# Eight matmuls without a use taken out of TensorE's queue between attention and experts, in a vision-tower kernel

## The reference, cut to what matters

```
h = tok(x)                                   # conv patches, local attention, class query: (64, 5, 256)
h = concat([cls_tok, h], axis=1)             # six tokens
h = h + attn(layernorm(h))                   # 16 heads, causal, ALiBi
x2 = layernorm(h)
logits = x2 @ gate_w                         # 8 experts, top 2
hidden = silu(x2 @ gate_w_e) * (x2 @ up_w_e) # for every expert e
h = h + sum over the top two of p_e * (hidden_e @ down_w_e)
```

## Time and profile before

| what | value |
|---|---|
| median of 3 runs | 247.56 us |
| the runs | 247.16, 247.56, 248.78 us |
| profiled execution: span, first to last instruction | 245.7 us |
| median less that span: what lies around it | 1.9 us |
| mean granted TensorE clock over the span | 0.971 |
| TensorE busy / its weight loads | 203.7 / 187.4 us |
| VectorE, ScalarE, GpSimd busy | 169.6, 105.8, 98.2 us |

### The profile page before, as it was taken

One profiled execution on the slowest core, in us unless ns is written; L12 is line 12 of the kernel. 1 busy time (PEld: TensorE's weight loads), 2 busy tenths in 40 slices (PEclk: granted clock), 3 DMA queues, 4 the chain that ended last, 5 costly groups with the idle time before them and its releaser, 6 DMA issues.

```text
span 245.7 us, 3903 instructions
## 1 busy us (share of the span) xinstructions
PE 203.7 (83%) x1320; PEld 187.4 (76%) x1320; DVE 169.6 (69%) x365; ACT 105.8 (43%) x230; POOL 98.2 (40%) x99
## 2 busy tenths in 40 slices
PE   0279899499999794687868899999999999999950
PEld 0279888379898574565646789999999999999950
DVE  0454895988464899967888769497857695948420
ACT  2153875172626560434321147364728372534200
POOL 0003879939414296337446404243322341514000
PEclk9999999859999997999999999999999999999996
DMA  6749933000930000000000001553543336000031
GB/s 198 239 125 365 379 153 128 23 1 0 366 149 0 0 1 3 0 0 0 1 0 3 0 0 40 220 184 98 234 124 132 104 152 236 20 0 0 3 18 46
DMA packets 5494, 23.01 MB, mean 94 GB/s; under 512 B 454, under 2 KB 3176, under 8 KB 4328
## 3 DMA queue, kind: packets, MB, share of 16 engines
q1 hardware_dynamic: 3746, 21.20, 24.6%
q10 hardware_dynamic: 1734, 1.63, 2.1%
HBM read 22.44 MB, written 0.39 MB: 93 GB/s over the span
## 4 chain that ended last, share of the span: by engine, by line
PE 57%; DVE 18%; issue 8%; POOL 5%; DMA 4%; ACT 3%; ACTq 1%; DVEq 0%; POOLq 0%
PE bank L720 22%; PE bank L733 14%; PE bank L420 8%; DMA raw<-xb 4%; PE bank L473 4%; DVE kv_rows L1191 2%; PE bank L610 2%; DVE vprod L344 2%; POOL rstd L1003 2%; POOL split L1032 2%; DVE normed L1160 1%; PE bank L619 1%; POOL window L1017 1%; DVE stats L1146 1%; PE bank L442 1%
## 5 line engine op out<-in xcount | busy, mean ns | idle before, releaser
L720 PE MATMUL bank<-split 128*128 128x322 f32 x384 | 59.2, 314 | 0.6 <-DVE normed L1517 0.6
L720 PEld LDWEIGHTS bank<-split 128*128 128x128 f32 x384 | 57.6, 188 | 0.9 <-issue 0.9
L1131 POOL TENSOR_TENSOR split<-raw,split 128x256 fp32r<-128x256 f32 x32 | 28.9, 905 | 56.7 <-DVE split L1470 56.7
L733 PE MATMUL bank<-split 128*128 128x256 f32 x288 | 36.1, 283 | 0.6 <-DVE split L1523 0.6
L733 PEld LDWEIGHTS bank<-split 128*128 128x128 f32 x288 | 35.4, 192 | 0.8 <-DVE split L1523 0.8
L420 PE MATMUL bank<-split 128*128 128x256 f32 (+1 forms) x255 | 34.0, 295 | 2.1 <-DVE split L1260 1.3
L420 PEld LDWEIGHTS bank<-split 128*128 128x128 f32 (+1 forms) x255 | 32.8, 203 | 2.6 <-issue 1.6
L473 PE MATMUL bank<-split 128*128 128x512 f32 x108 | 28.3, 417 | 0.4 <-DVE split L1292 0.4
L473 PEld LDWEIGHTS bank<-split 128*128 128x128 f32 x108 | 21.2, 201 | 5.0 <-DVE split L1292 0.7
L974 ACT ACTIVATE normed<-bank 128x322 f32<-128x322 f32 x32 | 13.9, 436 | 23.6 <-PE bank L720 23.6
L1517 DVE TENSOR_TENSOR normed<-bank,normed 128x322 f32<-128x322 f32 x32 | 15.7, 491 | 11.3 <-PE bank L720 8.0
(11 more groups left out here) (164 smaller groups left out, 292.8 us busy)
## 6 DMA issues: line engine op xcount, KB each, us to landing
raw<-ffn_w SPq DMA_DIRECT2D x8, 1536.0 KB, 6.5
raw<-xa SPq DMA_DIRECT2D x5, 768.0 KB
tok<-tok_w SPq DMA_DIRECT2D x1, 1536.0 KB, 11.9
tok<-tok_w SPq DMA_DIRECT2D x1, 776.0 KB, 7.5
raw<-xb SPq DMA_DIRECT2D x5, 114.0 KB
raw<-conv_w SPq DMA_DIRECT2D x1, 512.0 KB
raw<-xa ACTq DMA_DIRECT2D x1, 512.0 KB
att<-att_w SPq DMA_DIRECT2D x1, 488.0 KB, 12.7
```

What stands on the lines that cost most here:

```text
L720: mm = pe.matmul(bank[b][:, 0:NCOL], aws[:, q, pw, a:a + P], ms[:, px, c, FIRST:ROWS], start=(c == 0 and m == 0), stop=(c == CC - 1 and m ...
L733: mm = pe.matmul(bank[b][:, 0:C], hids[:, px, s * FQ + q, a:a + P], bws[:, s, pw, q * C:(q + 1) * C], start=(q == 0 and m == 0), stop=(q = ...
L1131: pool.tensor_tensor(bws[:, s, LO, q * C:(q + 1) * C], b_raw[:, s, q, :], bws[:, s, HI, q * C:(q + 1) * C].bitcast(F32), ALU.subtract).the ...
```

## The change

The helper `keep_clock` and its three calls are taken out, eight matmuls of the program in all, sixteen MATMUL records. Nothing else differs.

```
-            def keep_clock(b, n):
-
-                for _ in range(n):
-                    pe.matmul(bank[b][:, 0:C], ident, wp[:, 0, :], start=True, stop=True)
-
...
             pe.wait_ge(gstep, 5)
             two_chunk(7, "gproj", gaggT, gproj)
-            keep_clock(6, 4)
             turn_in(2)
             tile_qkv(2, "qkv_pool")
...
             router(0, 3)
-            keep_clock(6, 2)
             router(1, 2)
             turn_mid(2, 5)
-            keep_clock(6, 2)
             router(2, 5).then_inc(filled[4], 1)
```

## The result

| what | before | changed |
|---|---|---|
| median of 20 runs | 247.79 us | 250.91 us |
| lowest, highest | 246.09, 250.26 us | 248.09, 253.05 us |
| ratio to before | | 1.0086, 95% interval 1.0055 to 1.0117 |
| span of the profiled execution | 245.7 us | 248.4 us |
| mean granted clock over it | 0.971 | 0.939 |

The kernel is slower by 0.9%: some 2.1 us by the ratio, 2.7 us between the two profiled executions, 3.1 us between the medians. The ratio leaves out runs over 1.5% above the fastest of their kernel, six of the changed kernel's (mean granted clocks of 0.933 to 0.940, its lowest) and one of the kernel before, so it is not the quotient of the medians and may be a little low. The forecast was 249.0 us, +1.4 us.

The account below looks back on a forecast made before the run. TensorE was busy 203.7 of 245.7 us with 57% of the chain; the changed part was a chain of short steps between four engines. Terms -0.1 + 0.8 + 0.7 = +1.4 us gave 249.0 us, range 247.0 to 251.6.

Parts of the forecast that it names:

- the case held likeliest: Clock falls for a short stretch in the attention and again at the router: 249.0 us, chance 0.40.
- The direct term: Queue time freed on TensorE by taking the eight matmuls out: -0.1 us, low end -0.2.
- The first place: Wait before the turning of token row 2: clock falls at about 126 us for 3.4 us, +0.8 us.
- the bound of +2.4: Upper bound before token row 2's turning and behind it: low stretch lasts 6.8 us and catches context 1 too.
- The router: Without its two pairs the clock falls about when the experts begin, slowing their first 24 matmuls: +0.7 us.
- The forecast's +3.2: Upper bound at the router: a 6.8 us low stretch slows all first 24 expert matmuls, 3.8 us less 0.6.
- The sum: All terms over the profiled execution: -0.1 + 0.8 + 0.7 = +1.4 us, span 245.7 to 247.1.
- The third rival: Low stretches last 6.8 us: 250.6 us (attention only), 251.5 (router only), up to 253.1 (both); chance 0.20.
- Only the first place: Clock falls in the attention only; thin matmuls hold it at the router: +0.7 us, 248.3 us, chance 0.23.
- No fall: Clock holds in the attention and at the router; only freed queue counts: -0.1 us, 247.5 us, chance 0.17.

## Why the prediction was right, and where its sizes were off

The mechanism was right at both places: the dummies cost next to nothing in TensorE's queue, and the clock falls without them. The sizes were not: the case held likeliest, both low stretches short, is not what the profile shows, and the measured time is within the range because the range has room for one long stretch.

**The direct term**, -0.1 us. The run without the router's pairs shows -0.08 us from context 2 to router 2, the changed kernel -0.16, a part of which may be the delay running out in waits. Of the half microsecond by which a pair holds router 1 back, the turning of mid row 2 lets nearly nothing through, as said.

**The first place**, +0.8 us. The wait became 3.56 us (3.57 forecast) and the clock was low for 3.4 us. TensorE was late by 1.39 us at output projection 0 (1.30 and the 0.09 of the start; 1.4 forecast), by 1.22 at context 1 (1.1) and by 0.77 at context 2 (0.8). Step for step this is as forecast, for an execution like the profiled one. What was not: the first call alone measured +0.85%, 2.1 us (0.9 to 3.2), nearer to the bound of +2.4. Its runs' mean clocks show a longer low clock in eight of twelve, where the profiled one is the fastest; how much of the difference this makes stays open.

**The router**, +0.7 us: mis-sized. It measured +2.17 us in the profiled execution. The forecast let the low clock begin shortly before the experts and last 3.4 us. It began at 143.1, with router 2 (143.17), and lasted 6.8 us. The first 0.61 us are router 2 itself, 1.44 in place of 0.83; a cost the forecast had no term for. The rest is the first expert: from its first gate-up to its first down projection 13.46 us (144.47 to 157.93) against 11.90 (143.34 to 155.24), +1.56. The forecast's +3.2 for such a long stretch was too much, on three counts. The stretch ended at 149.97, when twenty of the first 24 records had started; each took 0.27 us from its start to the next against 0.15 at the full clock, 1.8 times and not twice; so the 24 took 6.26 us against 3.84, +2.42 in place of +3.8. And 0.86 of it did not reach the first down projection, where 0.6 was taken off for the wait of 0.63 us before the third gate-up, which was used up as forecast. By time over many runs this place is smaller again, 0.4%.

**The sum.** -0.09 for an earlier start, +0.77, -0.16 from context 2 to router 2, +0.61, +1.56 make the 2.69 us between the last instructions. The third rival, long stretches at the router, is the one that the profiled execution shows (251.5 us forecast for it, 250.2 measured in that execution). The measured ratio, +0.9%, lies between it and the likeliest case. Against this rival the forecast held that the waits after 126 us are 0.57 us and less; that was misread, for before router 0 TensorE waits 0.78 us (139.09), and before the third gate-up 0.63.

**The rivals.** "Only the first place" fell by the run without the router's pairs: by the Trainium skill ("TensorE: Matmul & The Clock Gate", section "Why this matters for your kernels") it is idle gaps that bring the clock down, and the longest at the router was 0.92 us; it fell all the same, and here the measurement decides. "No fall" is refuted by the profiles of the changed kernel and of both single removals. Of the forecast's other place in the Trainium skill (the same page, section "Part 1: The HAM clock gate (the "warmup" mystery)"), that the ramp costs under 1% of a kernel's span: the cost that this change adds stays below that, at 0.86%, with an interval that reaches to 1.17%; what the low clock costs the whole kernel was not measured.

## What to carry to other kernels

A matmul without a use can earn its place: in a chain of short steps much of what a slow clock costs one engine reaches the end, and here 4 us of dummies in or near waits save some 2 us. What they stream and how many there are matters: four of 256 columns ahead of the last token's turning were worth it, two were not, and neither were twice as many of eight columns. Before adding more, look whether TensorE is on the chain there. And one profiled execution doesn't tell in how many others the clock falls: compare the mean clocks of all runs too.

## What the runs showed that was not expected

A group of sixteen eight-column records looks in the timeline just as busy as one of eight 256-column records, 1.85 against 1.89 us, but the clock fell behind it. And a low stretch moved: filled at 47 and 95 us, it came back at 100 and 127 us, with the time unchanged. The calls of the kernel before are no warrant: with the first in place the clock still fell at 127 us in one profiled execution, with the router's two pairs in place at 141 us in another, both of kernels with filled waits. Even where nothing was changed the stretches differ between executions: the one at 95 us lasted 3.4 us before and 6.8 us in the profile of the kernel with seven matmuls in the first call, which is the same up to there.
